# A decoder layer with self and cross attention on one core: queries and keys projected feature-major for pairs of tiles, without dense transposes

## The reference

```python
h = _ln(x, ln1_g, ln1_b)
q = (h @ sa_wq + sa_bq).reshape(Bx, Lx, H, HD) * scale      # H = 16 heads, HD = 16
k = (h @ sa_wk + sa_bk).reshape(Bx, Lx, H, HD)
v = (h @ sa_wv + sa_bv).reshape(Bx, Lx, H, HD)
q = _apply_rope(q, cos[:Lx], sin[:Lx]); k = _apply_rope(k, cos[:Lx], sin[:Lx])
x = x + (_attn(q, k, v, causal=True).reshape(Bx, Lx, E) @ sa_wo + sa_bo)
h = _ln(x, ln2_g, ln2_b)                                    # cross: q from h, k and v from y, both rotated,
...                                                         # no mask; x = x + (a @ ca_wo + ca_bo)
h = _ln(x, ln3_g, ln3_b)
x = x + (gelu(h @ fc1_w + fc1_b) @ fc2_w + fc2_b)           # FF = 1024
ti = softmax(y @ x.T) ...                                   # second part: rows of x attend the context
out = tanh(concat([x, ti]) @ trans_W + trans_b) + x
```

## Time and profile before

| | |
|---|---|
| median of 3 runs | 3020.07 us (3018.67 to 3022.89) |
| profiled execution | 3020.76 us, its span 3019.0 us |
| instructions | 92928 |
| mean granted clock of TensorE | 0.987 of full speed |
| HBM read, written | 56.62 MB, 16.78 MB |
| first load of the loop | 76.65 us from the span's start |

### The profile page before, as it was taken

The page is one execution under the profiler, slowest core; times in us unless marked ns, Lnnn a source line. Parts: engine busy times, 40 slices in busy tenths (PEclk is TensorE's granted clock), DMA queues, the critical chain, the costliest instruction groups (busy, mean ns, idle before and its releaser), DMA issues.

```text
span 3019.0 us, 92928 instructions
## 1 busy us (share of the span) xinstructions
PE 2857.9 (95%) x38860; PEld 2447.0 (81%) x38860; DVE 2451.2 (81%) x5319; ACT 2043.0 (68%) x4481; POOL 1446.1 (48%) x2180
## 2 busy tenths in 40 slices
PE   3699999999999999999999999999999999999997
PEld 2478888888888888888888888888888888888876
DVE  4598888888888888888888888888888888888873
ACT  0267676776776777767777677777776777776765
POOL 0354454544554555445554554455544544554431
PEclk7799999999999999999999999999999999999999
DMA  3222212222122122221221222212212222122110
GB/s 83 56 51 50 51 46 51 50 50 53 46 51 50 46 52 49 49 53 46 50 51 47 51 49 50 53 46 50 51 46 52 49 49 54 46 50 51 39 30 17
DMA packets 242932, 148.63 MB, mean 49 GB/s; under 512 B 40616, under 2 KB 242216, under 8 KB 242512
## 3 DMA queue, kind: packets, MB, share of 16 engines
q1 hardware_dynamic: 242512, 142.68, 19.9%
HBM read 56.62 MB, written 16.78 MB: 24 GB/s over the span
## 4 chain that ended last, share of the span: by engine, by line
PE 58%; ACT 17%; DVE 15%; DMA 5%; SPq 2%; issue 2%; POOL 1%; POOLq 0%; DVEq 0%; ACTq 0%
ACT pt_c L1042 7%; PE sc L400 7%; PE A L374 6%; PE A L375 6%; PE A L376 6%; DMA qkt_c<-qkst_c 5%; PE A L465 5%; ACT L1042 5%; PE B L597 4%; PE B L375 3%; PE A L369 3%; PE B L374 3%; PE B L376 3%; PE B L603 3%; DVE ct_lo L721 2%; PE A L581 2%
## 5 line engine op out<-in xcount | busy, mean ns | idle before, releaser
L1199 POOL TENSOR_TENSOR rstd<-bmv,eps_t 128x1 f32<-128x1 f32 x384 | 118.7, 309 | 740.8 <-DVE bmv L920 472.2
L1194 POOL TENSOR_TENSOR qkf_s<-tqk,rope_c 128x512 f32<-128x512 f32 x128 | 165.3, 1291 | 546.2 <-DVE tqk L727 546.2
L1042 ACT ACTIVATE pt_s<-sc 128x512 f32<-128x512 f32 x512 | 264.6, 604 | 100.0 <-PE sc L390 100.0
L1201 POOL TENSOR_TENSOR rstd<-rstd,mhalf 128x1 f32<-128x1 f32 x384 | 295.0, 768 | 30.1
L743 DVE TENSOR_REDUCE z_s<-sc 128x8 f32<-128x1024 f32 x256 | 301.7, 1221 | 7.1
L743 DVE TENSOR_REDUCE z_c<-sc 128x8 f32<-128x1024 f32 x256 | 296.6, 1197 | 1.4 <-PE sc L400 1.4
L1042 ACT ACTIVATE pt_c<-sc 128x512 f32<-128x512 f32 x512 | 264.4, 603 | 7.5 <-PE sc L400 6.1
L1204 POOL TENSOR_TENSOR kr_c<-qkt_c,ones_f 128x512 bf16<-128x512 f32 x128 | 137.7, 1076 | 169.8 <-DMA qkt_c<-qkst_c 169.8
L1032 ACT COPY x3t<-B 128x256 f32<-128x256 f32 x128 | 47.7, 373 | 203.6 <-PE B L369 203.6
L1083 ACT ACTIVATE vaug_s<-B,rstd 128x256 f32<-128x256 f32 x128 | 60.9, 476 | 158.8 <-PE B L376 158.7
L1048 ACT ACT_TABLE_LOAD x128 | 164.2, 1283 | 2.3
(11 more groups left out here) (226 smaller groups left out, 10907.9 us busy)
## 6 DMA issues: line engine op xcount, KB each, us to landing
qkt_s<-qkst_s SPq DMA_DIRECT2D x256, 128.0 KB, 2.5
qkt_c<-qkst_c SPq DMA_DIRECT2D x256, 128.0 KB, 2.6
xt_f<-in_x_t SPq DMA_DIRECT2D x128, 128.0 KB, 2.1
rows_in<-in_x SPq DMA_DIRECT2D x128, 128.0 KB, 2.2
rows_in<-in_ctx_t SPq DMA_DIRECT2D x128, 128.0 KB, 2.4
out<-o_out SPq DMA_DIRECT2D x128, 128.0 KB, 1.7
qkt_s<-zt_s SPq DMA_DIRECT2D x512, 2.0 KB
qkt_c<-zt_c SPq DMA_DIRECT2D x512, 2.0 KB
```

The lines of the kernel that those rows point to most:

```text
L1042: act.activation(pt[c][:, r, :, :].rearrange("p g q -> p (g q)"), sc[:, r, :], ACT.Exp).then_inc(signal, 1)
L1194: pool.tensor_tensor(out.rearrange("p (h e) -> p h e", e=HD), t[:, :].rearrange("p (h e) -> p h e", e=HD), rope_c[:, :].unsqueeze(1).broad ...
L1201: pool.tensor_tensor(rstd[k - 1][:, :], rstd[k - 1][:, :], mhalf[:, :], ALU.pow).then_inc(s[f"rstd{k}"], 1)
```

## The change

Queries and keys are now projected feature-major. `pair_projection` keeps the weight stationary and streams the features of two tiles, so features come out on partitions and no transpose is needed. In one slot `sq_` gives the queries of a pair of tiles, in the next its keys, 12 matmuls of 256 columns each time; `cp_` does the same for cross attention (keys, then queries). The columns of the four weights are reordered on the host, all first halves of the heads ahead of all second halves, so the rotation swaps two column blocks. The bias is per partition and is added by ScalarE (`tq_s_`, `tq_c_`, two activations of 256 each). The scale by the reciprocal deviation can no longer be per partition: for layer norm 1 the row of 128 values goes to a DRAM buffer (`rbw_`) and comes back on all partitions (`rbr_`), and VectorE multiplies x_t by it ahead of the split (`xs_`); for layer norm 2 ScalarE scales x1 ahead of its transpose (`x2n_`). Both spreads take eight DMAs per call (32 partitions, 2 tiles of 128 values each) instead of two. `cvt_` gives the context's values and its product with trans_W in one pass, six matmuls 512 wide. The context is loaded a second time for the last part (`ld_g_`), with smaller rings for the loads. The setup has eight and twelve small DMAs for the constant rows of `qkt`, which now has four buffers, instead of four and six. All slot orders and many delays are new: the pipeline runs for u = 0 to 142.

```diff
-            transposes(A0, qkf["s"][:, :], G).then_inc(s["trqk_s"], 1)
...
-            transposes(B0, qkf["c"][:, :], G).then_inc(s["trqk_c"], 1)
...
+            def pair_projection(bank, w, c0, a_hi, a_lo):
+                for h in range(2):
+                    c = c0 + h
+                    for k in range(KC):
+                        mm = split3(bank[:, h * E:(h + 1) * E], w_hi[w][:, k, c * P:(c + 1) * P], w_lo[w][:, k, c * P:(c + 1) * P],
+                                    a_hi[:, k, :], a_lo[:, k, :], k == 0, k == KC - 1)
+                return mm
...
+            def spread(c, t, first, landed):
+                b = (t - 1) // M % 2 * M
+                for h in range(2):
+                    for g in range(G):
+                        sp.dma_start(qkt[c][2 * h:P:4, b:b + M, first + g, :],
+                                     rp[c][32 * g:32 * g + 32, h * E:(h + 1) * E].rearrange("p (j q) -> p j q", j=M)).then_inc(landed, 16)
...
+            def dq_s_(t):
+                if live_pair(t):
+                    sp.wait_ge(s["add_s"], pairs(t))
+                    spread("s", t, 0 if t % 2 == 1 else G, dq_s[t % 2])
...
+            def rbw_(t):
+                    sp.wait_ge(s["rs1"], done(t))
+                    sp.dma_start(rstd_rows[t % 4].unsqueeze(1), rstd1[t % 2][:, :]).then_inc(rbw[t % 2], 16)
...
+            def rbr_(t):
+                    sp.wait_ge(rbw[t % 2], 16 * (t // 2 + 1))
+                    sp.dma_start(rb[t % 2][:, :], rstd_rows[t % 4].partition_broadcast(P)).then_inc(rbr[t % 2], 16)
...
+            def sq_(t):
+                    pair_projection(B0, "sqk", 2 * ((t - 1) % M), xt_hi, xt_lo).then_inc(s["sq"], 1)
...
+            def kr_s_(t):
+                    if t % 2 == 0:
+                        need(pool, dq_s[(t + 2) % 2], 128 * ((t + 2 + 1) // 2))
+                    rounded("s", t)
...
+            def y_s_(t):
+                    need(pe, s["ghia"], pairs(t - 5))
+                    project("s", B0)
```

More of the change, by code:

```diff
@@ L153, in build @@
         st_hi, st_badd = sem("st_hi"), sem("st_badd")
-        ld_x = [sem(f"ld_x{i}") for i in range(R)]
+        ld_x = [sem(f"ld_x{i}") for i in range(RX)]
         ld_t = [sem(f"ld_t{i}") for i in range(RT)]
         ld_c = [sem(f"ld_c{i}") for i in range(RC)]
+        ld_g = [sem(f"ld_g{i}") for i in range(RG)]
+        rbw = [sem(f"rbw{i}") for i in range(2)]
+        rbr = [sem(f"rbr{i}") for i in range(NB["rb"])]
         st_o = [sem(f"st_o{i}") for i in range(2)]
-        dqk_s, dqk_c = [[sem(f"dqk_{c}{i}") for i in range(2)] for c in "sc"]
+        dq_s, dq_c = [[sem(f"dq_{c}{i}") for i in range(2)] for c in "sc"]
@@ L159, in build @@
         zd_s, zd_c = [[sem(f"zd_{c}{i}") for i in range(2)] for c in "sc"]
[L160 to L166, removed]
+        names = ("st1", "mv1", "eps1", "rs1", "xs", "xt_hi", "xt_lo", "vs", "v_s", "sq", "tq_s", "cos_s", "rot_s", "add_s",
+                 "qr_s", "kr_s", "p1s", "max_s", "zt_s", "p2s", "exp_s", "pv_s", "ot_s", "rinv_s", "att_s", "norm_s",
+                 "xres_s", "y_s", "x1", "st2", "mv2", "eps2", "rs2", "x2n", "xres_c", "trx2", "x2t_hi", "x2t_lo",
+                 "ct_hi", "ct_lo", "cvt", "v_c", "cw", "cp", "tq_c", "cos_c", "rot_c", "add_c",
+                 "qr_c", "kr_c", "p1c", "max_c", "zt_c", "p2c", "exp_c", "pv_c", "ot_c", "rinv_c", "att_c", "norm_c",
+                 "y_c", "x2", "st3", "mv3", "eps3", "pow3", "neg3", "rs3", "xh3", "x2b", "trx3", "h3_hi", "h3_lo",
@@ L329, in _ @@
+            steps(slot, 15)
             for q in st_o:
@@ new lines, in trfa_, with trx3_, fy0_ @@
+            def trfa_(t):
+                if live(t):
+                    pe.wait_ge(s["fatt"], done(t))
+                    need(pe, s["cw"], done(t + 8))
+                    pe.transpose(A0[:, 0:P], fexp[:, :], ident[:, :]).then_inc(s["trfa"], 1)
+            def trx3_(t):
+                if live(t):
+                    pe.wait_ge(s["xh3"], done(t))
+                    need(pe, s["ot_s"], done(t + 5))
+                    transposes(B0, xhat[:, :], KC).then_inc(s["trx3"], 1)
+            def fy0_(t):
+                if live(t):
+                    for k in range(KC):
+                        mm = pe.matmul(A1[:, 0:E], x3t[t % 1][:, k, :], w_t1[:, k, :], start=(k == 0),
+                                       stop=False, skip_group_check=True)
+                    mm.then_inc(s["fy0"], 1)
@@ L1052, in xt_hi_, with gelu @@
+            def gelu(t, bank, p, out):
+                for cc in range(2):
+                    c = 4 * (1 - t % M) + 2 * p + cc
+                    w = act.activation(out[:, cc, :], bank[:, cc * M * P:(cc + 1) * M * P], ACT.Gelu_apprx_tanh,
+                                       bias=bias_f1[:, c:c + 1])
+                return w
             def xt_hi_(t):
                 if live(t):
[L1054 to L1055 removed]
@@ L1188, in _ @@
+                x2n_(u - 3)
+            steps(slot, 15)
         @block.gpsimd
```

1236 lines of the change are left out of this document (589 added, 647 removed).

## The result

The changed kernel takes **3849.56 us** (median of 4 runs, 3839.97 to 3881.0) against 3021.48 beside it (4 runs, 3018.67 to 3024.17): a ratio of 1.276, 95% interval 1.268 to 1.283. The forecast was 2935, the range 2830 to 3045, and slower had a chance of 0.21. The profiled execution took 3854.4 us, its span 3852.3.

What follows compares the result with a forecast made beforehand. TensorE, busy 95% of the span, was taken as the bound: 20.88 us of work plus 0.65 of stall gives 21.5 per tile, 0.85 less. 3020.8 - 120 x 0.85 + 16 = 2935 us, range 2830 to 3045.

Steps and rivals of the forecast that it cites:

- the round trip: Scaling of x through DRAM (rs1, rbw, rbr, xs): cost nothing, at most one late landing, 1 us.
- some 5 us of issues: SyncE's queue: rbw issued ahead of the eight dq_c, whose issues cover rbr's wait for the write.
- It is full, but not over: SyncE's queue: 16 spreads, 8 for maxima and 7 others take 17 us of 21.5 per tile.
- TensorE's work: TensorE's stream per tile: 21.89 less 0.91 for transposes and 0.10 for groups, leaving 20.88 us.
- I take -0.1: TensorE, context values and product in one pass: one group fewer saves 0.1 us per tile, bounds 0 and -0.2.
- The stall of p1s: Self scores waiting for kr_s: 1.3 us late every second slot, +0.65 us per tile, bounds none and 1.8.
- Rival A: p1s waiting for kr_s behind dq_s: the spread chain becomes the bound, 22.7 us per tile, 3079 us; chance 0.12.
- Rival B: ScalarE's order meets TensorE's, y_s after both gelua passes: 0.85 us more per slot, 3037 us; chance 0.06.
- Rival C: Weight loads pace TensorE, which gains nothing: 22.35 us per tile or more, 3037 us; chance 0.02.
- VectorE: VectorE's work per tile: about two full-width instructions less, 1.3 us, from 18.9 to some 17.5.
- The ends: Setup's extra small DMAs +4 us and a pipeline three slots deeper +12 us, bounds 0 and 33.
- The range: 2830 to 3045 us, from the lower bound past B and C, leaving out nearly all of A.

Runs made afterwards that it cites:

- e1: Changed kernel without the DRAM write and read of the reciprocal deviation, x multiplied by ones, layer norm 1 scaling left out: 3272.8 us.
- e10: Whole changed kernel, rstd column first turned into rows by a VectorE transpose, so the write is 4 pieces of 128 bytes: 3440.4 us.
- e2: Changed kernel with the round trip's write and read issued by GpSimd instead of SyncE: 4136.8 us.
- e4: Changed kernel with statistics, rstd and its write one slot earlier, the read at the slot's head, ld_t ahead of the self spread: 3587.4 us.
- e6: e1 with the write of 128 pieces of 4 bytes per tile kept, nobody reading it back: 3811.2 us.
- b2: Kernel before the change, plus one unread DRAM write per tile of 128 pieces of 4 bytes from a constant: 3315.6 us.
- b1: Kernel before the change, each spread issued as eight DMAs of 32 KB instead of two of 128 KB: 3560.7 us.
- e5: Changed kernel without the round trip (as e1) and with only four of the eight DMAs of each spread issued: 3034.2 us.
- e8: e6 with the same 512 bytes written as 4 pieces of 128 bytes from a tile of ones: 3318.1 us.

## Why the prediction was wrong

**The step that failed** is the round trip: "Its cost is taken as nothing, bounded by -0 and one late landing, 1 us." It costs 577 us (e1), some 4.3 us per tile (28.4 less 24.1), four times its bound. I priced it as a latency under the cover of "some 5 us of issues". What I priced is real and the smaller part: with few pieces it costs 168 us (e10 against e1). The larger, 409 us, is the write's shape, 128 pieces of 4 bytes. It lands 7.3 us after its issue in e2. In the changed kernel SyncE still waits for it in 44 slots, 124 us in all, and in those the read goes out 7.0 to 10.1 us behind the write, so the cover was too short as well. The transfers behind it are late too (e4, e6, b2). No row of the trace before had a DMA of such pieces; the landings I had read were of spreads of 128 KB. The upper bound should have been open, with every transfer behind the write in SyncE's queue counted as late.

**The second step that failed** is "It is full, but not over." The issue price was right: 0.58 forecast, 0.607 median. The arithmetic of 17 us in 21.5 would do for a queue that runs freely (e1's issues add up to 17.3 us per tile), and this queue does not: its issues are links of loops. The self spread is issued only after add_s, and ld_t, rbr and the maxima stand behind both spreads. Halving the issues takes 385 us off the change, or 239 off e1 (3272.8 to 3034.2), 2.0 us per tile; and in the kernel before, whose issues take 8.8 us per tile, twelve more bring them to 16.5, well under 22.35, and cost 539 us (b1).

**TensorE's work**: the transposes went and sq takes 1.44 us in one piece, as forecast. But in e5, at a full clock, TensorE is still busy 21.6 us per tile and not 20.88. The seams between groups took the gain back. Timeline of the kernel before, a feed-forward group of 12 matmuls up to the next group:

```profile
1504.79 0.28 PE L374 MATMUL C<-w_f_hi,hid_hi_b 128*128 128x256 f32 x1
...
1506.15 0.38 PE L369 MATMUL A<-ident,xhat 128*128 128x128 f32 x2
```

The same kind of group in e5:

```profile
1801.05 0.39 PE L393 MATMUL C<-w_f_hi,hid_hi_a 128*128 128x256 f32 x1
...
1802.57 0.40 PE L393 MATMUL A<-w_cvt_hi,ct_hi 128*128 128x512 f32 x1
```

1.36 us before, 1.52 now. Before, this group followed a projection; now it follows scores of 128 columns, and its second matmul starts 0.23 us after the first instead of 0.11. Taken the same way, the four feed-forward groups go from 5.73 us (1.36, 1.49, 1.42, 1.46) to 6.27 (1.52, 1.52, 1.71, 1.52), and the two output projections from 1.64 to 1.93: 0.83 us, nearly what the transposes gave. The projections of the cross attention with the context's product fall from 3.19 to 3.01, so "I take -0.1" for one group fewer was sound; what failed is that all other groups kept their old price in the sum, while the new order gave them new neighbours.

**The stall of p1s** in every second slot is there (the wait of the scores for kr_s: 179 us in all, 31 of them once in the fill; the rest is 1.2 per tile, where 0.65 was forecast and 1.8 was the bound). The place was right; it is not where the time went. What was short in its sum is VectorE: from the rotation's start to the end of add_s 3.6 us pass (2030.80 to 2034.36) where 2.0 were allowed, since ct_lo stands between them and the sum takes 1.5.

**Rival A** had the right side and the right kind (issues and landings of the spreads on a chain), with a price of 3079 us: its place, p1s behind dq_s, is one of three. **Rival B** falls: ScalarE's work is 16.9 us per tile (16.8 forecast), and in e5 TensorE idles 0.5 us per tile, its longest wait for ScalarE being 39 us in all (xhat), where B needed 0.85 per slot. **Rival C** can't be the loss, since weight loads are busy 68% of the span here against 81% before. No run took it apart from the seams in e5, where the loads are at 80%; against it stands what stood before, 256-wide matmuls 0.12 us apart. That e5 comes out at 3034, beside the 3037 of B and C, proves neither. The Trainium skill's rule (Perfetto Trace Analysis, "Identifying the Most-Contended Engine") takes the loads' share, not the matmuls', to say how close TensorE is to its roofline. By either (68% or 80%) TensorE is the most contended engine here, and the trace puts the bound elsewhere: SyncE's issues have 32% of the chain, TensorE 19%. **VectorE**: forecast 17.5 us per tile, measured 19.1, no less than before. add_s takes 1.49 us on average instead of 0.68, with GpSimd at work beside it; the two were not taken apart. The ends cost some 40 us more in e5 (span less 128 periods of 22.1 to 22.2 us: 195 to 205, before 158), where +16 was forecast.

**The range** was not built by its own bounds: the lower end takes 0.2 us more off the groups where 0.1 was left of the bound, and the upper end takes a stall of 1.2 us where the bound was 1.8, which would give 3098. Neither comes near 3850.

**The sum**: forecast 2935; the seams (a period of 22.1 for 21.5) and the longer ends make it 3034 (e5); the spreads' issues 3273 (e1); the round trip's two landings 3440 (e10); its 128 pieces 3850.

What stays open: by which resource the small pieces hold up the later transfers. The runs show that issues behind the write stall up to 4.3 us and landings are late, with the 16 DMA engines' mean busy share at 0.20; they don't show where the pieces queue. The DMA packets in the traces narrow it: packets of 1 KB (loads of rows and stores) that last over 1.5 us come 233 times in the middle of the changed kernel, 322 in e6 and 429 in b2, never in the kernel before, e1 and e8, and once in e10. The instruction fetches, which are on other queues, lengthen with them (100 such packets in the changed kernel, 7 in e1), while half of all 4-byte packets last 9 ns or less. So the hold-up isn't confined to SyncE's queue. How the 0.8 us of seams would fall with another order wasn't tried either.

## What to carry to other kernels

Count the pieces of a DMA, not its bytes: a column of 128 partitions by 4 bytes written to DRAM cost microseconds to itself and to what was issued behind it here, and a transpose of 0.21 us on VectorE that makes it 4 pieces removed most of that. A queue whose issues wait for results and release them is a link of a loop and not a resource with a busy share: write the loop down once round, with every issue in it, before calling 17 of 21.5 us enough. When all orders are new, price the seams of the slow engine's stream again, and remember that a stall on TensorE is paid a second time in its clock.

## What was not expected of the hardware

- 512 bytes written as 128 pieces of 4: 7.3 us to landing (e2), and +538 us over 128 tiles with nobody reading (e6); as 4 pieces of 128 bytes, +45 (e8).
- A single issue on SyncE's queue behind such a write took up to 4304 ns (e6), against a median of 607 and a longest of 1837 without the write (e1).
- After 3.50 us of idle time TensorE was granted 0.50 of its clock, and twelve 256-wide matmuls took 2.72 us instead of 1.44.
- VectorE and GpSimd side by side on 128x512 tiles in SBUF: the sum rp_s took 1.52 us against 0.66 for a like operation before, the cosines 1.80 against 1.29. That one slows the other is read from the timelines, not tried. Tile rp_s of the changed kernel, min, median and max in ns:

```profile
L1188 POOL TENSOR_TENSOR rp_s<-tq_s,rope_c x128: 1270/1802/1819, 119.0 to 3692.0; 128x512 f32<-128x512 f32 x128
L738 DVE TENSOR_TENSOR rp_s<-rp_s,rw_s x128: 678/1524/1528, 120.8 to 3694.0; 128x512 f32<-128x512 f32 x128
```
